# Recurrence and expert layer on eight cores: filler matmuls spread evenly over the scan steps, and two row blocks per output store

## What is computed

```python
xn = _layernorm(x)
u  = einsum('bsd,nd->bsn', xn, Wi) + bi
sp = einsum('bsd,nd->bsn', xn, Ws) + bs
state = tanh(state @ A.T + u_t @ B.T) + sp_t        # for every token, in order
y_t = state @ C.T
attn = einsum('bsn,dn->bsd', ys, Wo) + bo
logits = xn @ router_weight                         # 8 experts, the best two, softmax
gate = minimum(gate, 7); up = clip(up, -7, 7)
act = (up + 1) * gate * sigmoid(1.702 * gate)
ffn = sum over experts of w * (act @ down_proj)
out = x + attn + ffn
```

## Time and profile before

| | us |
|---|---|
| median of 2 runs | 1679.52 (1679.38 to 1679.66) |
| the profiled execution | 1679.23 |
| its span, core 6, the slowest | 1677.7 |
| spans of the eight cores | 1665.6 to 1677.7 |
| PE busy in the span | 1487.6 |
| DVE busy | 903.1 |
| ACT busy | 559.6 |

### The profile page before, as it was taken

How to read it: one execution, slowest core, us unless ns; L and a number is a source line. 1 busy time by engine, 2 the same in 40 slices (tenths; PEclk the granted TensorE clock), 3 DMA queues, 4 the chain that set the end, 5 groups by cost and what they waited for, 6 DMA issues and landing times.

```text
span 1677.7 us, 25847 instructions; the slowest of 8 cores (1665.6 to 1677.7 us)
## 1 busy us (share of the span) xinstructions
PE 1487.6 (89%) x6944; PEld 670.2 (40%) x6998; DVE 903.1 (54%) x2133; ACT 559.6 (33%) x1013; POOL 120.6 (7%) x230
## 2 busy tenths in 40 slices
PE   0445988699999999999999999999999999999983
PEld 0221444214444444444444444444444444444432
DVE  4553666433466446644664466546653665366543
ACT  3442233450355035502551255115511552155200
POOL 2000000000000000000000000000000000000011
PEclk9766999859999999999999999999999999999995
DMA  5410111102222222221222122212222222222058
GB/s 130 112 38 1 26 26 26 26 0 32 32 39 38 45 32 38 39 40 30 39 39 44 26 40 41 42 31 39 39 44 32 38 39 45 32 39 39 14 101 225
DMA packets 36314, 74.66 MB, mean 45 GB/s; under 512 B 4864, under 2 KB 4864, under 8 KB 36176
## 3 DMA queue, kind: packets, MB, share of 16 engines
q0 software_dynamic: 31424, 55.71, 21.8%
q1 hardware_dynamic: 4752, 17.30, 3.0%
HBM read 120.10 MB, written 8.39 MB: 77 GB/s over the span
## 4 chain that ended last, share of the span: by engine, by line
PE 81%; DVE 6%; DMA 5%; ACT 3%; issue 3%; DVEq 0%; ACTq 0%; POOL 0%; another core or an unknown queue 0%; POOLq 0%; SPq 0%
PE pb L287 26%; PE pb L868 26%; PE pb L277 24%; DMA xres<-xm 1%; DVE etu L313 1%; DMA y<-otm 1%; ACT et L326 1%; PE pb L743 1%; PE pb L738 1%; PE pb L481 1%; DVE acc L884 1%; PE pb L695 1%; DVE etg L318 1%; PE pb L493 1%; ACT G L704 1%
## 5 line engine op out<-in xcount | busy, mean ns | idle before, releaser
L277 PE MATMUL pb<-xn_fm,wgu 128*128 128x512 bf16 x2048 | 496.7, 384 | 2.5 <-ACT wbc L658 1.0
L287 PE MATMUL pb<-xn_fm,wgu 128*128 128x512 bf16 x2048 | 490.7, 381 | 0.1
L868 PE MATMUL pb<-act_w,wdb_ 128*128 128x512 bf16 x2000 | 446.1, 382 | 9.7 <-DVE acc L884 5.9
L884 DVE TENSOR_TENSOR acc<-acc,pb 128x512 bf16<-128x512 bf16 x256 | 176.0, 688 | 277.6 <-PE pb L868 275.0
L868 PEld LDWEIGHTS pb<-act_w,wdb_ 128*128 128x128 bf16 x2048 | 201.1, 98 | 253.5 <-issue 17.4
L277 PEld LDWEIGHTS pb<-xn_fm,wgu 128*128 128x128 bf16 x2048 | 198.4, 99 | 242.9 <-issue 19.6
L287 PEld LDWEIGHTS pb<-xn_fm,wgu 128*128 128x128 bf16 x2048 | 198.0, 98 | 232.2 <-issue 5.1
L307 ACT CAST etu<-pb 128x512 bf16<-128x512 f32 x224 | 131.0, 585 | 255.9 <-PE pb L287 255.9
L326 ACT ACTIVATE et<-etg 128x512 bf16<-128x512 bf16 x256 | 161.2, 630 | 77.3 <-DVE etg L318 43.3
L305 ACT CAST etg<-pb 128x512 bf16<-128x512 f32 x224 | 131.1, 585 | 93.4 <-PE pb L277 92.5
L321 DVE TENSOR_SCALAR etu<-etu,sbu 128x512 bf16<-128x512 bf16 x256 | 91.9, 359 | 110.0 <-ACT etu L307 104.4
(11 more groups left out here) (105 smaller groups left out, 513.6 us busy)
## 6 DMA issues: line engine op xcount, KB each, us to landing
wgu<-Wg POOLq DMA_DIRECT2D x64, 256.0 KB, 3.5
wgu<-Wu POOLq DMA_DIRECT2D x64, 256.0 KB, 3.5
wdb_<-Wd POOLq DMA_DIRECT2D x64, 256.0 KB, 3.5
xln<-xm SPq DMA_DIRECT2D x16, 512.0 KB, 3.7
y<-otm SPq DMA_DIRECT2D x16, 512.0 KB, 5.4
xres<-xm POOLq DMA_DIRECT2D x16, 256.0 KB, 5.8
xln<-xw SPq DMA_DIRECT2D x1, 512.0 KB, 4.9
sWiT<-WiT POOLq DMA_DIRECT2D x1, 256.0 KB, 6.1
```

The lines of the kernel that those rows point to most:

```text
L277: e.matmul(bg_[:, 0:STW], wgu[:, 2 * par, dc, :], rhs, start=(dc == 0), stop=(dc == NDC - 1)),
L287: e.matmul(bu2[:, 0:STW], wgu[:, 2 * par + 1, dc, :], rhs, start=(dc == 0), stop=(dc == NDC - 1)),
L868: e.matmul(bk[:, 0:STW], wdb_[:, par, ic, :], act_w[:, ic, stt * STW:(stt + 1) * STW], start=(ic == 0), stop=(ic == NDC - 1), skip_group_c ...
L884: e.tensor_add(acc[:, fc, stt * STW:(stt + 1) * STW], acc[:, fc, stt * STW:(stt + 1) * STW], bk[:, 0:STW]),
```

## The change

Two edits. `pump` is called with 2 in all steps, where it was 4 in the first 16. And the output is stored once per two row blocks: the DMA is issued after the second block's add, covers both halves of `otm` and 256 rows of `y` (1 MB), and always uses s_ou0; each add waits for the store of the pair before (from mc = 2 on).

```diff
@@ -667,7 +667,7 @@
                 if PH < 2: raise _Done()
                 ch_act = {}
                 for s in range(NSTEP):
-                    pump(4 if s < 16 else 2)
+                    pump(2)
                     b = s % 2
                     if b == 0:
                         for k in range(2):
@@ -780,7 +780,7 @@
                     for mc in range(stt * 4, stt * 4 + 4):
                         par = mc % 2
                         par4 = mc % 4
-                        fosem = "s_ou%d" % par
+                        fosem = "s_ou0"
                         fxsem, lxv = fxload[mc]
                         bank = pbt[par]
                         tvals = []
@@ -797,7 +797,7 @@
                             tvals.append(t_)
                         vwl = [("s_te", tvals[7]), (fxsem, lxv)]
                         if mc >= 2:
-                            vwl.append((fosem, out_done[par]))
+                            vwl.append((fosem, out_done[mc // 2 - 1]))
                         ve(lambda e, bank=bank, par=par, par4=par4:
                            e.tensor_add(otm[:, par, :], bank[:], xres[:, par4, :]),
                            wait=vwl)
@@ -805,8 +805,12 @@
                         fin_add[par4] = cnt["s_ve"]
                         if mc + 4 < NMC:
                             emit_final_load(mc + 4)
-                        out_done[par] = dma("sy", fosem, d_y[mc * 128:(mc + 1) * 128, :],
-                                            otm[:, par], wait=[("s_ve", fin_add[par])])
+                        if par == 1:
+                            dst3 = d_y[(mc - 1) * 128:(mc + 1) * 128, :].rearrange(
+                                "(s p) c -> p s c", s=2)
+                            out_done[mc // 2] = dma(
+                                "sy", fosem, dst3, otm[:],
+                                wait=[("s_ve", fin_add[par])])
 
 
                 if PH < 4: raise _Done()
```

## The result

The changed kernel takes 1686.47 us (median of 11 runs), the kernel before 1678.86 in the 10 runs beside it. The ratio is 1.0048, with an interval of 1.0038 to 1.0058: 8 us slower, well within 2%, and yet told apart from no change. I compare core 6 with core 6; its span went from 1677.7 to 1682.6 us (core 1 ends last now, at 1683.4).

A forecast was written before the change was run, and what follows sets the result against it. Expert matmuls are untouched; the recurrence is bound by its steps and filler, the output stage by transfers and their waits. 1679.2 - 11.5 + 17.8 = 1685.5 us, 0.4% slower; 8 in 10 range 1668 to 1696.

The forecast's parts named there:

- both its parts: Recurrence: filler spread to the last step, 11.5 us less; output stage: one 1 MB store per pair, 17.8 us more.
- the waits that it named: Output stage: both adds of a pair wait for the whole previous pair's store; a cycle is adds plus landing, 9.4 us.
- L714 starts earlier: End of the recurrence: L714 starts at 323.4 instead of 334.88, 11.5 us less, with 2 us allowed each way.
- L714 to the first add: Stages between recurrence and output: keep their length; 2 us allowed for the clock's short drops coming at other moments.
- first add to last landing: Output stage: the last store lands at 1694.9 against 1677.1, 17.8 us more.
- rival 2: Attention stage: clock stays at 2.4 GHz, ACT bounds, 8 us saved, kernel at 1677.5; chance 0.08.
- The store's landing: Output stage: a 1 MB store beside xres loads lands in 6.5 us, bounds 3.9 and 7.8.
- a sign of being wrong: Output stage: store landings near 4 us or above 8 would show the forecast wrong.
- Rival 1: Output stage: the big store is hardly hindered, landing 3.9 us throughout, kernel ends at 1670; chance 0.20.
- Rival 3: Output stage: a merged store lands as two contended ones in sequence, 13.0 us, kernel at 1724.5; chance 0.04.
- The reason that I gave for 6.5: Output stage: the second of two neighbouring stores already queues behind the first; a pair is that in one piece.
- The prediction's sum with one load's turn: Output stage: a store waits for about one load's turn, 3.9 and 2.0, so the sum would end near 1682.

The follow-up runs named there:

- e1: Kernel before with only the filler edit, pump(2) in all steps, stores as before: median 1667.1 us, ratio 0.9918 to before.
- e2: Kernel before with only the store edit, one 1 MB store per two row blocks: 1701.9 us, ratio 1.0120 to before.
- e5: Changed kernel with all xres loads issued during the last expert's down projection, into xn_fm: 1679.0 us, ratio 0.9992 to before.
- e10: Changed kernel with xres loaded early: four blocks during gate and up projections, the others two behind each weight load: 1669.0 us, ratio 0.9932 to before.
- e9: Filler edit alone with old stores, plus xres loaded early: four blocks during gate and up, the others two behind each weight load: 1651.4 us, ratio 0.9829.
- e4: Changed kernel with four halves of otm instead of two; 1 MB stores stay, adds wait for the pair before the last one: ratio 0.9917 to before.
- e7: Kernel before with eight filler matmuls a step in the first 4 steps only, four after (pump(4 if s < 4 else 2)): one run, 1669.93 us.
- e8: Kernel before with pump(4) throughout, eight filler matmuls a step until used up after 64 steps: one run, 1705.94 us.
- e3: Changed kernel with each pair's store cut into two of 512 KB after their own adds, still waiting for the whole pair before: ratio 1.0002 to before.
- e6: Filler edit alone with old stores, all xres loads issued during the last expert's down projection, into xn_fm: 1662.0 us, ratio 0.9886 to before.

## Why the prediction was right

It said 1685.5 and the median is 1686.47; the mechanism held, both its parts and the waits that it named, but for the reason that it gave for the landing's size (below). That the sum came within 1 us is in part luck. The filler edit alone gained 13.8 us where the prediction had 11.5 (e1, 0.82%), and the store edit alone cost 20.2 where it had 17.8 (e2, 1.20%): each was sized some 2.4 us too small, and in the sum the two cancel. It also called 2% about what a measurement can tell from no change; the interval of the result is 0.1% either way. On core 6, the profiled executions give its terms one by one:

| term | predicted | measured |
|---|---|---|
| L714 starts earlier | -11.5 | -11.9 |
| L714 to the first add | 0, at most 2 either way | -2.3 (1289.5 to 1287.2) |
| first add to last landing | +17.8 | +19.3 |

These sum to +5.1 on core 6 where the forecast had +6.3; its errors of -0.4, -2.3 and +1.5 partly cancel here as well. The ratio of the medians, of each run's slowest core, is worth 8.

- The recurrence held step by step: tanh 4 at 168.8 (168.6 said), tanh 96 at 280.2 (280.3), tanh 127 at 319.7 (320.1), L714 at 323.0 (323.4). On cores 0, 2 and 3 of before the recurrence took 173.3 us, and the edit gives 10.4 and not 12; they lack the drop of the clock to 0.50 for 3.4 us that the other five show at about 198 us.
- The attention stage kept its low clock: rival 2 is out.
- The store's landing was the estimate with the widest bounds, 3.9 to 7.8 with 6.5 taken. It measured 6.65 on core 6. One of the six took 8.43, just past the 8 that the prediction had named as a sign of being wrong; the mean did not. From the first store's issue at 1613.69 to the seventh's at 1671.22 the six cycles are 9.6 us each, where the sum had 9.4: 1.1 of the 1.5 us missed, the end of the stage the rest. Rival 1 asked for 3.9, which appears only when the loads are gone (e5, e10: 4.0 to 4.4). Rival 3 asked for 13.
- The reason that I gave for 6.5, that a pair is two neighbouring stores in one piece, was not the right one. Without loads, neighbouring stores of 512 KB land in 2.7 us in the median (e9), and 1 MB takes 4.1 (e5). What adds the 2.5 us is the loads, in the changed kernel the two that the same adds release. By the Trainium skill ("DMA: Bandwidth & Descriptors", Queues, rings and completion order) the engines take the queues in turn. The prediction's sum with one load's turn gave 5.9, and measured were 6.65; that part of the second load is served too would fit, and no row shows it.
- The middle stretch is the term that I had put at nothing. Five cores of before have 1289.4 and more there and three 1286.7; in the changed kernel all eight lie between 1286.7 and 1287.2. The work is the same. The windows around the end of expert 0's down projection show what differs: before, core 6 had a short drop of the clock there (0.72 over 6 us) and core 0 had none at the same place.

```profile
434.00:440.00 6.00, 5.39 (x18) 1.89 (x18) 0.35 (x1) 2.34 (x4) 0.00 (x0) 0.72 0.30 44
```

```profile
426.00:432.00 6.00, 5.62 (x26) 2.56 (x27) 1.00 (x3) 3.21 (x6) 0.00 (x0) 1.00 0.26 43
```

The clock records of all cores bear this out. Behind the attention stage, each core of before, changed, e1, e2, e4 and e7 to e10 has either four drops to 0.50 of 3.4 us each, and then 1286.5 to 1287.5 us, or five, and then 1289.3 to 1290.8. The changed kernel has four on all eight cores; before, cores 0, 2 and 3 have four and the others five. On core 6 the slow clock around the attention stage also ended 45.4 us behind L714 before and 44.0 now. As an estimate from these records, at half the clock a drop of 3.4 us costs 1.7 us and those 1.4 us more of slow clock 0.7, together 2.4 us; measured were 2.3. What decides between four and five drops stays open: e7, whose recurrence ends 1.5 us later, has five on all cores, and in e8 cores with the same recurrence of 201.4 us have 1286.5 and 1290.0.

## What to carry to other kernels

Merging two stores saved an issue that nobody waited for and made every buffer come free later; here it was harmless only with buffers for one transfer more (e4). To estimate a wait for a transfer, count what else the same event releases onto the DMA engines, beside the transfer's own bytes. Filler beside a chain of dependent steps belongs spread to its last step: a bare step costs its latency whatever stood ahead of it (e8). The fastest kernel here (e9) also moved loads out of the stage in which adds and stores wait for them.

## What I had not expected

- Beside two loads, a store of 512 KB that followed its pair's first half took 5.4 to 7.9 us to land (e3), one of 1 MB 5.2 to 8.4. Without loads they took 2.7 in the median (e9; the longest 4.9) and 4.0 to 4.4.
- Taking 12 loads out of the output stage made it 15 us shorter (55.0 to 39.5), although they are loads that run ahead of their use by four blocks.
- With three loads behind each weight load the middle stretch was 8 us longer than with two (e6 and e9; e9 also moves the first four loads ahead), and POOL's order of time shows weight loads issued late.
- A stretch of 1287 us that the edit does not touch took 2 to 3 us more or less, with five short drops of the clock in it or four.
